# The stages between attention and experts, ordered for each engine by a planner, with routing in wider steps

## What is computed

```
x = layernorm(x + attention16(x))            # 16 heads, causal, with a distance penalty
x = layernorm(x + real(ifft(fft(x) @ w)) + bias)
x = layernorm(x + channel_attention(x))      # 8 heads; scores are between channels
x = layernorm(x + experts(x))
```

```
qkv = x @ w_qkv + b_qkv
scores = einsum('bhld,bhle->bhde', q, k) / sqrt(dx)
out = einsum('bhld,bhde->bhle', v, softmax(scores)) @ w_fc + b_fc + x
out = (out - mu) * rsqrt(var + EPS) * gamma + beta
```

```
aff = x @ centroids.T
eid = argmax(aff)
h = relu(xln @ w1[eid] + b1[eid])
out = x + sigmoid(sum(x * centroids[eid])) * (h @ w2[eid] + b2[eid])
```

## Time and profile before

| | us |
|---|---|
| median of 3 runs | 1555.1 |
| lowest and highest | 1551.25 and 1556.09 |
| the profiled execution | 1549.12 |
| its span | 1547.1 |
| TensorE, busy in the span | 1417.8 (92%) |
| VectorE | 1076.7 (70%) |
| ScalarE | 854.5 (55%) |
| GpSimd | 240.9 (16%) |
| middle: first Turn to last PlaceRows | 966.65 to 1235.91 |
| first matmul with w1 of the experts | 1255.10 |

### The profile page before, as it was taken

How to read it: one execution, slowest core, us unless ns; L and a number is a source line. 1 busy time by engine, 2 the same in 40 slices (tenths; PEclk the granted TensorE clock), 3 DMA queues, 4 the chain that set the end, 5 groups by cost and what they waited for, 6 DMA issues and landing times. The chain is left out here.

```text
span 1547.1 us, 43841 instructions
## 1 busy us (share of the span) xinstructions
PE 1417.8 (92%) x18356; PEld 858.0 (55%) x18356; DVE 1076.7 (70%) x1993; ACT 854.5 (55%) x1783; POOL 240.9 (16%) x380
## 2 busy tenths in 40 slices
PE   7878999999999999999999999898977559999998
PEld 4434444444444444444444453786754259999997
DVE  2376768888887888878888871554558647677675
ACT  2335647767677677676776767552425323433333
POOL 3212021011101111021111110000112611111111
PEclk9999999999999999999999999897998779999999
DMA  8574018513215113142300000570032254554541
GB/s 234 158 120 91 22 64 120 66 26 49 34 28 68 27 30 47 28 59 28 88 3 3 4 2 2 190 257 7 1 98 79 76 208 171 182 186 178 186 175 71
DMA packets 77823, 134.09 MB, mean 87 GB/s; under 512 B 12226, under 2 KB 64443, under 8 KB 72252
## 3 DMA queue, kind: packets, MB, share of 16 engines
q1 hardware_dynamic: 72412, 121.45, 30.4%
q0 software_dynamic: 3408, 8.43, 1.6%
q10 hardware_dynamic: 1808, 1.41, 0.3%
HBM read 67.77 MB, written 23.11 MB: 59 GB/s over the span
## 5 line engine op out<-in xcount | busy, mean ns | idle before, releaser
L1512 DVE TENSOR_REDUCE part_max<-pair 128x2 f32<-128x1024 f32 (+2 forms) x576 | 647.5, 1162 | 115.3 <-PE pair L982 57.4
L1334 ACT ACTIVATE big<-pair 128x512 f32<-128x512 f32 (+1 forms) x1120 | 565.2, 610 | 239.7 <-PE pair L1003 237.4
L976 PE MATMUL pair<-big 128*32 128x512 bf16 (+3 forms) x5120 | 359.6, 352 | 29.1 <-DVE part_max L1512 24.2
L1003 PE MATMUL pair<-big 128*32 128x512 bf16 (+3 forms) x5120 | 345.1, 351 | 3.4 <-issue 1.4
L1025 PE MATMUL pair<-big 128*17 128x512 f32 (+3 forms) x2560 | 280.3, 528 | 2.7 <-issue 2.3
L976 PEld LDWEIGHTS pair<-big 128*32 128x32 bf16 x5120 | 135.1, 97 | 198.4 <-DVE part_max L1512 98.8
L1003 PEld LDWEIGHTS pair<-big 128*32 128x32 bf16 x5120 | 126.8, 96 | 174.3 <-ACT big L1334 88.7
L1347 ACT ACTIVATE std<-moments,eps_col 128x1 f32<-128x1 f32 (+1 forms) x110 | 32.5, 295 | 261.6 <-DVE moments L1550 261.6
L1878 POOL TENSOR_SCALAR_AFFINE_SELECT big<-big 128x512 f32<-128x512 f32 x128 | 80.0, 637 | 474.3 <-ACT big L1334 474.3
L1242 PEld LDWEIGHTS pair<-big,tok 128*128 128x128 f32 x1248 | 147.8, 195 | 4.9 <-DVE big L1778 3.0
L1242 PE MATMUL pair<-big,tok 128*128 128x128 f32 x1248 | 148.3, 278 | 2.4 <-DMA tok<-big 1.4
(11 more groups left out here) (163 smaller groups left out, 1279.0 us busy)
## 6 DMA issues: line engine op xcount, KB each, us to landing
tok<-big SPq DMA_DIRECT2D x39, 1024.0 KB
big<-in_L_ffn_w SPq DMA_DIRECT2D x16, 1024.0 KB, 12.3
big<-split_dram SPq DMA_DIRECT2D x216, 64.0 KB, 4.6
split_dram<-big SPq DMA_DIRECT2D x32, 384.0 KB, 2.7
big<-split_dram SPq DMA_DIRECT2D x42, 256.0 KB, 6.1
big<-routed_dram SPq DMA_DIRECT2D x39, 129.0 KB, 2.1
tok<-in_L_attn_x SPq DMA_DIRECT2D x8, 512.0 KB, 9.2
big<-in_c_query_rows SPq DMA_DIRECT2D x8, 512.0 KB, 5.3
```

The source lines that it names most:

```text
L976: mm = pe.matmul(bank[q:q + STRIPE, o:o + w], m.q_op[slot][:, step.qt, h, step.r * P + q:step.r * P + q + STRIPE], m.k_op[slot][:, h, step ...
L1003: mm = pe.matmul(m.bank[step.bank][k:k + STRIPE, n * w:(n + 1) * w], m.k_op[slot][:, h, step.kb * P + k:step.kb * P + k + STRIPE], m.q_op[ ...
L1334: act.activation(m.p_ring[:, step.place, step.heads[0]:step.heads[-1] + 1, step.at:step.at + w], m.bank[step.bank][:, 0:len(step.heads) * ...
L1512: dve.tensor_reduce(m.part_max[(step.u * QT + step.qt) % 2][:, step.r, step.heads[0]:step.heads[0] + n, step.c], banks[:, :, 0:w], X, ALU. ...
```

## The change

`BackPlan` becomes a planner with a clock for each engine. Every step has a cost in ns, and at each turn the step that can start first on its engine is taken; each engine gets a list of its own (`plan.pe`, `plan.act`, `plan.dve`, `plan.pool`, `plan.sp`). The joint steps are split (Multiply and Add; Moments, Roots, Shift and End). The order of stages is no longer written down: a Turn is chosen from those that are possible. The fold's steps come when their inputs are due.

```diff
-C_ORDER = "O0 O1 O2 O3 S0 S1 O4 S2 S3 O5 O6 S4 O7 S5 S6 S7"
-GRAM_STEP, FOLD_LAG, ROUTE_LAG = 2, 3, 1
+ROUTES = [(0, 1), (2, 3), (4, 5), (6,), (7,)]
+SCATTERS = 8
...
+    LAG, PE_LAG = 80, 190
+    TURN, COPY, MULTIPLY, ADD, MOMENTS, ROOTS, SHIFT, APPLY = 1050, 600, 3500, 720, 2050, 320, 550, 2100
+
     def __init__(self):
...
+        self.now = {"pe": 0, "act": 0, "dve": 0, "pool": 0}
+        self.pe, self.act, self.dve, self.pool, self.sp = [], [], [], [], [Experts(True)]
+        self.done = {"loaded": 9000}
...
+        if stage == "O":
+            free = max(free, 6000 if g < 2 else self.done["add", "O", g - 2] + 6000)
...
+        if stage == "O" and g + 2 < TILES:
+            self.sp.append(Residual(g + 2, 2 * m + 2))
...
+    def step(self):
+        choices = []
+        for engine, sources in (("pe", (self.turn_choices(), self.use_choices())),
+                                ("act", (self.copy_choices(), self.root_choices(), self.end_choices())),
+                                ("dve", (self.add_choices(), self.norm_choices(), self.shift_choices(),
+                                         self.second_choices())), ("pool", (self.beta_choices(),))):
+            for source in sources + (self.fold_choices(engine), self.route_choices(engine)):
+                choices += [(max(ready, self.now[engine]), rank, len(choices) + i, take, what)
+                            for i, (ready, rank, take, what) in enumerate(source)]
...
+        _, _, _, take, what = min(choices, key=lambda choice: choice[:3])
+        take(*what)
```

```diff
-            for c in range(KC):
-                mm = pe.matmul(m.bank[step.bank][0:EXPERTS, :], m.cent_t[:, c, :], m.turned_x[slot][:, c, :],
-                               start=(c == 0), stop=(c == KC - 1))
+            for r in range(BPT):
+                o = ((step.g - tiles[0]) * BPT + r) * EXPERTS
+                for c in range(KC):
+                    mm = pe.matmul(m.bank[AFFINITY_BANKS[step.route]][:, o:o + EXPERTS], m.turned_x[slot][:, c, r * P:(r + 1) * P],
+                                   m.cent_t[:, c, :], start=(c == 0), stop=(c == KC - 1))
             mm.then_inc(s.turn_used, 1)
```

The first three copies of w1 go ahead of the fetches of rows, each after its own third of the scatters:

```diff
+    sp.wait_ge(s.expert_set, 1)
+    sp.wait_ge(s.experts_in, 16 * 2 * EXPERTS)
+    for i in range(W1_AHEAD):
+        sp.wait_ge(s.scatter[i], 16 * SCATTERS)
+        fetch_w1(i)
     sp.wait_ge(s.rows_set, 1)
-    sp.wait_ge(s.expert_set, 1)
-    sp.wait_ge(s.scatter, 16 * BLOCKS)
+    for scatter in s.scatter:
+        sp.wait_ge(scatter, 16 * SCATTERS)
     sp.wait_ge(s.pads_out[0], 16 * EXPERTS // 2)
     sp.wait_ge(s.pads_out[1], 16 * EXPERTS // 2)
-    sp.wait_ge(s.experts_in, 16 * 2 * EXPERTS)
     for i in range(ROWS_AHEAD):
         fetch(i)
-        if i <= W1_AHEAD - 1:
-            fetch_w1(i)
     fetch_w1(W1_AHEAD)
```

More of the change, by code:

```diff
@@ L503, with affinity_before @@
-PadTile = namedtuple("PadTile", "used")
+NormParams = namedtuple("NormParams", "m")
+PadTile = namedtuple("PadTile", "m")
+def affinity_before(route):
+    return max((i for i in range(route) if AFFINITY_BANKS[i] == AFFINITY_BANKS[route]), default=None)
 class BackPlan:
+    LAG, PE_LAG = 80, 190
+    TURN, COPY, MULTIPLY, ADD, MOMENTS, ROOTS, SHIFT, APPLY = 1050, 600, 3500, 720, 2050, 320, 550, 2100
     def __init__(self):
[L510 to L524, removed]
-        before = {"S": "O", "C": "S", "A": "F"}.get(stage)
[L526 to L538, removed]
@@ L539, in multiply @@
+    def multiply(self, n, stage, g, ready):
         m = self.n_multiply
         self.n_multiply += 1
[L541 to L546, removed]
@@ new lines, in norm_choices @@
+    def norm_choices(self):
+        i = self.n_norm
+        last = self.at(("end of", i - 2)) if i >= 2 else 0
+        if last is None:
+            return
+        for stage in "OSCF":
+            for g in range(TILES):
+                if (stage, g) in self.norm_of:
+                    continue
+                ready = self.at(("second", g) if stage == "F" else ("add", stage, g))
+                if ready is not None:
+                    yield max(ready, last), 2, self.moments, (i, stage, g, max(ready, last))
+                    break
@@ L659, in back_plan @@
-    plan.n_job += ROUTE_LAG
-    take(plan.routes, 10 ** 6)
+    while plan.step():
+        pass
+    assert not plan.todo and plan.fold is None
     return plan
@@ L1354, in scalar_back @@
     act.wait_ge(s.vector_set, 4)
-    for step in plan.steps:
-        if isinstance(step, Turn):
+    for step in plan.act:
+        if isinstance(step, Copies):
             for c, b in enumerate(TURN_BANKS):
@@ L1587, in vector_back @@
     dve.wait_ge(s.chosen_set, 1)
-    for step in plan.steps:
-        if isinstance(step, Multiply):
+    for step in plan.dve:
+        if isinstance(step, Add):
             g = step.g
@@ L1885, in pool_back @@
     pool.memset(m.ones_b, 1.0).then_inc(s.onesb_set, 1)
-    for step in plan.steps:
+    for step in plan.pool:
         if isinstance(step, Parameters):
@@ L2129, in program @@
     back.front_ring = front.ring_at
-    back.o_multiply = next(step.m for step in back.steps
-                           if isinstance(step, Multiply) and (step.stage, step.g) == ("O", TILES - 1))
     with ExitStack() as ctx:
```

521 lines of the change are left out of this document (314 added, 207 removed).

## The result

| | kernel before | changed kernel |
|---|---|---|
| median of 5 runs each, us | 1551.82 | 1562.91 |
| lowest and highest | 1550.62 and 1556.09 | 1561.44 and 1564.34 |
| span of the profiled execution | 1547.1 | 1559.7 |
| TensorE, VectorE busy | 1417.8, 1076.7 | 1410.2, 1070.0 |

The changed kernel takes 1.0074 of the time of the kernel before (95% interval 1.0057 to 1.0091): 11 us slower, with less work on both busy engines.

What follows compares the result with a forecast made beforehand. The limit changes by stretch: TensorE full, then folds almost alone, last a chain through VectorE and ScalarE. +0.8 to the last PlaceRows and +6.2 at the handover make +7.0 on 1555.1: 1562 us, range 1545 to 1580.

Steps and rivals of the forecast that it cites:

- Steps 1 and 2: Loads: residual behind weights holds O tile 2's Add until 1011.6, 19.6 us delay; then TensorE at half speed, +2.5.
- the rival's working: Residual passing the weights: O tile 3 ends 24.8 us earlier and 1.6 of half speed goes; chance 0.14.
- Steps 3 to 6: Stall to end of fold 1: fold 0 starts 1056.5, takes 40; Grams 33.0; fold 1 34, ending 1163.5.
- Step 7: Fold 1's end to last PlaceRows: 54.2 us of VectorE work at share 0.74, 73.2 us; end 1236.7, +0.8.
- Step 8: Handover to the experts: three w1 copies ahead of the first rows, landing at 1257.4 against 1251.24, +6.2 us.
- the faster rival: At O tile 2's Add: residual passes the weights, landing before about 986, TensorE never stands; -19, 1536; chance 0.14.
- The no-change rival: Last stage: planned order lifts VectorE's share from 0.74 to 0.83, 65 us, 8 less; -1, 1554; chance 0.23.
- the much slower rival: Both folds at upper ends (+4.8, +4.9) and, third, the last stage at VectorE share 0.66 (+8.8): 1580; chance 0.15.
- The meetings of VectorE with GpSimd's beta additions: GpSimd's eight beta additions beside VectorE's work: eight such pairs in both orders, counted as no difference.

Runs made afterwards that it cites:

- e1: Changed kernel with the experts' 11 early weights issued behind the residual of tile 5; 0.9902 of the kernel before, 26.6 us less than the changed kernel.
- e4: Kernel before with the 11 early weights issued ahead of the residuals of tiles 2 to 7; 1.0123 of the kernel before.
- e8: Changed kernel, weights still first on SP, residuals of tiles 2 to 7 issued by ScalarE on its own queue; 0.9914 of the kernel before.
- e10: e3 with matmuls on constants keeping TensorE busy around the Turns of F tiles 5 to 7; 0.9853 of the kernel before.
- e9: e3 with GpSimd's scatters of tiles 4 to 6 held until the last tile's rows are placed; measured once, 1533.25 us.
- e2: Changed kernel with first rows loaded ahead of w1, alternating, as before the change; 1.0034 of the kernel before, 6.2 us less than the changed kernel.
- e3 again: The kernel of e3 measured once more, as base of the last group; 0.9848 of the kernel before.
- e7: e3 with eight routings of one tile each instead of three of two tiles and two of one; 0.9879 of the kernel before.
- e3: Changed kernel with both edits, weights behind the residual of tile 5 and rows ahead of w1; 0.9854 of the kernel before, 1525.7 us.

## Why the prediction was right, and where it was not

Forecast 1562, measured 1562.9, slower, and inside the range; by the ratio it is +11 against a forecast of +7.0, and from mark to end +10.1. That the two absolute times agree within 1 us is luck: the forecast was added to a median of three runs, 1555.1, and the median of five is 1551.8.

**Steps 1 and 2** held. The Add was forecast for 44.9 us behind the mark (1011.6 - 966.7) and began at 44.4; the end of O tile 3 for 48.1, and it came at 49.5, since its second half itself ran at half speed. e1 puts the stall at 28.2 us at the next milestone, 26.6 in time, where the rival's working had 24.8 + 1.6 = 26.4; e4 and e8 show its cause.

**Steps 3 to 6** held within 3 us each. Fold 0 starts at 89.7 (forecast 89.8) and takes 37.5 with its stages, not 40, below even the lower bound of 38.2: 33.68 of it is work, less than the pricing had. The Grams take 35.4 instead of 33, a little above their bound of 35, and fold 1 32.9 instead of 34. Fold 1 ends at 195.6 against 196.8.

**Step 7 failed, at "I take the share as it was".** The work was right (54.2 forecast, 53.89 in the trace), the share was 0.67 and not 0.74: 80.5 us instead of 73.2, near the bound of 82 that the text names. The price of this one choice is 7.3 us. The sentence that hid the cause is that TensorE's work for the affinities "lies beside VectorE's and counts nothing". I had noted that F tiles 5 to 7 all come behind C tile 7, but not followed it: TensorE then stands, its clock falls, and the last three tiles are its chain at half speed. e10 takes 5.5 us off that chain. The second thing that step 7 has at nothing are the late starts of Best and PlaceRows, 2.7 us each; e9, without them, is 5.6 earlier (248.8 - 243.2; 0.7 of it was there by the end of fold 1). How the 7.3 us divide between the two is not shown, since the share of 0.74 had some of both in it: over this stage the clock was 0.83 before and 0.70 after, and before, one PlaceRows began 3.5 us late (1227.54). And e10 shows that the last PlaceRows was hardly the bound: the scatters and the writes of empty rows were nearly as late, which step 7 does not mention.

**Step 8 was right in the term and wrong in its surroundings.** The order of w1 and rows costs 6.2 us by e2, as forecast, give or take the 3 us of that comparison. (Each of the three copies waits for a quarter of the scatters, eight of 32, not for a third.) But the rows landed only 3.9 us later behind the last PlaceRows than before (19.2 against 15.3). "The end of SP's writes of empty rows follows from the last PlaceRows as before (10.2 us later)" failed: they ended 7.8 later (1253.04 - 1245.25). These writes took 7.67 us before and 5.89 after, and their length is what step 8 took as given. The mark to count from is their end, since SP waits for their landing: the first rows land 5.1 us behind it before and 6.0 in e2, 11.4 with w1 first, so the order costs 5.5 to 6.3. The last scatter is the worse mark: with rows first the landing comes from 4.7 (e9) to 9.1 us (e3 again) behind it.

In sum: the last PlaceRows came 6.0 later than forecast (276.1 against 1236.7 - 966.7 = 270.0), the rows 2.3 earlier behind it (19.2 against 1257.4 - 1235.9 = 21.5), the first expert matmul follows the rows by 3.4 instead of 3.9, as w1 is there already, and the experts' stage is 0.2 shorter. 7.0 + 6.0 - 2.3 - 0.4 - 0.2 = 10.1, what the profiles show. The forecast was near partly because its two errors had opposite signs.

**The rivals.** The residual did not pass the weights, since both are of one queue; with two queues (e8) it did, and landed 20.8 us behind the mark, 987.5 in the prediction's frame, where the faster rival asked for about 986. The Trainium skill (DMA: Bandwidth & Descriptors, "Queues, rings and completion order") calls completion "not FIFO per issuing engine"; in both orders tried here (e4 and the changed kernel) the small load came behind the whole train. The no-change rival needed a share of 0.83; it went the other way. Of the much slower rival the third part came true, the first two did not. The meetings of VectorE with GpSimd's beta additions, counted as no difference, were none: three stretched VectorE operations before and three after, 4.5 and 4.3 us in all. Each of them has two inputs in SBUF; statistics beside an addition were not stretched.

## What to carry to other kernels

When a step of a plan is moved in a queue, price what is behind it in that queue, not the step: 11 MB of weights that nobody needs for some 280 us (975.19 to 1253.83) cost 27 us for standing ahead of half a megabyte, and the fix is the place in the list or another issuing engine. A busy share carried over from another order is not a price for the end of a stage: follow the last two or three tiles through every engine, at the clock that an engine has behind its wait, and through the scatters and writes behind them. And when an edit shortens a chain and the time stays, look for what was second, in the waits of the engine that goes on: here the last PlaceRows came 7.4 us earlier, and the writes of empty rows, begun 7.1 earlier, ended only 2.3 earlier.

## What the runs showed of the hardware that I had not expected

- VectorE's waits for TensorE can end late while GpSimd issues a long string of scatters: 2.7 us for Best and as much for PlaceRows in the changed kernel, 0.1 without scatters beside them (e9), and 0.1 with scatters in groups of four (e7).
- SP's four writes of empty rows took 4.43 us to issue in e3, 5.89 in the changed kernel, 7.67 before and 11.34 in e10. The number of scatters still to come does not decide it: in e9 fifteen were, and the writes took 4.36. The longest (e10, e4 with 9.32, before) began in the midst of a string of scatters without a pause. That the scatters are the cause is only argued.
- Four loads of 0.5 MB issued from ScalarE into the midst of 11 MB from SP landed in 11.5 to 14.5 us (e8), against 3.9 and 4.0 for two issued after it.
- The front, the same code in all kernels, differed by up to 7 us between profiled executions (961.9 to 969.2 at the mark): two profiles should be compared from a mark behind what they share.
